# Gate integers on ScalarE, every second half's up integers on VectorE, in the last stage of a decoder layer's gated feed-forward

## The reference

```
def act_qdq(x):
    scale = jnp.maximum(jnp.max(jnp.abs(x)) / qmax, 1e-12)
    return jnp.clip(jnp.round(x / scale), -qmax - 1.0, qmax) * scale
x = act_qdq(x)
up = act_qdq(x @ lpbq_dequant(w_up).T)
gate = act_qdq(x @ lpbq_dequant(w_gate).T)
sig = fixed_qdq_u16(jax.nn.sigmoid(gate))
gate = act_qdq(gate * sig)
o = act_qdq(gate * up)
return o @ lpbq_dequant(w_down).T
```

## Time and profile before

| | |
|---|---|
| median of 3 runs | 1257.77 us (1257.39 to 1261.47) |
| the profiled execution | 1256.11 us |
| its span | 1254.3 us |
| busy in the span: PE, DVE, ACT, POOL | 91%, 85%, 74%, 36% |
| the third pass, 1102.3 to 1171.2 | 68.9 us; busy PE 55.36, DVE 62.68, ACT 33.82, POOL 49.79 |

### The profile page before, as it was taken

The page is one execution under the profiler, slowest core; times in us unless marked ns, Lnnn a source line. Parts: engine busy times, 40 slices in busy tenths (PEclk is TensorE's granted clock), DMA queues, the critical chain, the costliest instruction groups (busy, mean ns, idle before and its releaser), DMA issues. The chain is left out here.

```text
span 1254.3 us, 28844 instructions
## 1 busy us (share of the span) xinstructions
PE 1137.2 (91%) x8658; PEld 843.2 (67%) x8658; DVE 1070.1 (85%) x2303; ACT 934.0 (74%) x3155; POOL 448.1 (36%) x463
## 2 busy tenths in 40 slices
PE   1589999999999999999999999999975998989498
PEld 1456666666667666766666766666543988778498
DVE  6259999999999999999999999999874559989698
ACT  1368888888888888888888888888742569855595
POOL 0223334433334433333433333443110007767343
PEclk9899999999999999999999999999986999999799
DMA  5000000000100000100000100010000000000133
GB/s 165 23 17 27 28 22 21 21 21 23 34 22 20 20 20 20 34 24 20 20 20 20 30 29 20 20 33 22 5 4 8 1 1 0 1 1 1 32 104 99
DMA packets 35059, 32.85 MB, mean 26 GB/s; under 512 B 4164, under 2 KB 34748, under 8 KB 35004
## 3 DMA queue, kind: packets, MB, share of 16 engines
q1 hardware_dynamic: 32704, 31.50, 8.4%
q10 hardware_dynamic: 2300, 0.66, 0.3%
HBM read 24.81 MB, written 7.34 MB: 26 GB/s over the span
## 5 line engine op out<-in xcount | busy, mean ns | idle before, releaser
L593 ACT ACTIVATE Px<-score 125x896 f32<-125x896 f32 x128 | 117.4, 917 | 89.4 <-PE score L1121 89.4
L574 ACT ACTIVATE Ps<-score,nmax_s 112x112 f32<-112x112 f32 x512 | 176.3, 427 | 4.0 <-DVE nmax_s L797 4.0
L585 ACT ACTIVATE Px<-score,nmax_h 125x112 f32<-125x112 f32 x512 | 172.6, 367 | 0.8 <-DVE nmax_h L790 0.8
L790 DVE TENSOR_REDUCE nmax_c<-score 125x8 f32<-125x896 f32 x128 | 136.2, 1064 | 13.6 <-PE score L1040 10.4
L574 ACT ACTIVATION_READ_ACCUMULATOR Ps<-score,nmax_s 112x1 f32 x512 | 144.3, 282 | 0.0
L759 DVE TENSOR_REDUCE Zc<-Px 125x8 f32<-125x896 f32 x128 | 137.9, 1077 | 5.7 <-ACT Px L593 2.1
L504 POOL TENSOR_TENSOR Kbd_hi<-Ks_hi,mask 128x448 fp32r<-128x448 f32 x64 | 63.9, 999 | 202.9 <-PE score L1040 137.5
L1132 PE MATMUL outX<-Px,Vn 125*32 125x224 f32 x1536 | 113.6, 368 | 7.2 <-DVE Vn L773 7.2
L585 ACT ACTIVATION_READ_ACCUMULATOR Px<-score,nmax_h 125x1 f32 x512 | 113.0, 221 | 0.0
L525 POOL TENSOR_TENSOR rstd<-vare,half 112x1 f32<-112x1 f32 x64 | 35.1, 548 | 177.0 <-DVE vare L882 177.0
L531 POOL TENSOR_TENSOR xb<-x_in,abo 112x256 f32<-112x256 f32 x32 | 23.7, 739 | 200.2 <-DVE r L868 200.2
(11 more groups left out here) (244 smaller groups left out, 3638.2 us busy)
## 6 DMA issues: line engine op xcount, KB each, us to landing
ctx_in<-in_ctx SPq DMA_DIRECT2D x32, 375.0 KB
x_in<-in_x SPq DMA_DIRECT2D x32, 112.0 KB, 2.0
x_scratch<-x SPq DMA_DIRECT2D x32, 112.0 KB, 1.9
x2T_all<-x_scratch SPq DMA_DIRECT2D x32, 112.0 KB, 2.1
out<-x2T_all SPq DMA_DIRECT2D x32, 112.0 KB, 1.9
raw_w_up<-in_w_up SPq DMA_DIRECT2D x1, 768.0 KB, 5.6
raw_w_down<-in_w_down SPq DMA_DIRECT2D x1, 768.0 KB, 7.4
raw_w_gate<-in_w_gate SPq DMA_DIRECT2D x1, 768.0 KB, 9.5
```

Of the source, the lines that this page charges most:

```text
L574: ins = act.activation(Ps[:, g, :], score[slot][0:L, h // QUAD, (h % QUAD) * L:(h % QUAD + 1) * L], ACT.Exp, bias=nmax_s[:, g:g + 1], accu ...
L585: ins = act.activation(Px[u % 2][:, h, :], score[SLOT_OF[f"C{u}"]][0:C, h // QUAD, (h % QUAD) * L:(h % QUAD + 1) * L], ACT.Exp, bias=maxim ...
L593: act.activation(Px[u % 2][:].rearrange("s (q h) l -> s q (h l)", q=2), score[SLOT_OF[f"C{u}"]][0:C, :, 0:QW], ACT.Exp).then_inc(exp_c, 1)
L790: dve.tensor_reduce(dst, score[SLOT_OF[f"C{u}"]][0:C, :, 0:QW].rearrange("s q (h l) -> s q h l", h=QUAD), AX.X, ALU.max, negate=True).then ...
```

## The change

- ScalarE's `up_integers` serves half 0 only; VectorE gets an `up_integers` for half 1, which reads `bank[1]` itself.
- `glu_integers` goes from VectorE to ScalarE, both halves. In group 0 ScalarE first waits for `scales_ready`.
- The count of finished up integers is split by half (`up_q_done[h]`), since two engines now raise it; TensorE waits for the half whose bank it will overwrite, GpSimd likewise.

```diff
--- before.py
+++ after.py
@@ -1397,7 +1397,8 @@
         up_maxed, up_ready, scales_ready = sem("up_maxed"), sem("up_ready"), sem("scales_ready")
         gate_q_done, sig_done, sig_q_done = sem("gate_q_done"), sem("sig_done"), sem("sig_q_done")
         glu_done, glu_maxed = sem("glu_done"), sem("glu_maxed")
-        glu_q_done, up_q_done, h_done, h_maxed = sem("glu_q_done"), sem("up_q_done"), sem("h_done"), sem("h_maxed")
+        glu_q_done, h_done, h_maxed = sem("glu_q_done"), sem("h_done"), sem("h_maxed")
+        up_q_done = [sem(f"up_q_done{h}") for h in range(2)]
         TURN = HG * P
         places = {"x": spare[1][:, TURN:TURN + P], "gate": spare[1][:, TURN:TURN + P], "up": spare[1][:, TURN:TURN + P],
                   "glu": spare[0][:, TURN:TURN + P], "h": spare[1][:, TURN:TURN + P]}
@@ -1426,7 +1427,7 @@
             def hidden(g, h):
 
                 pool.wait_ge(glu_q_done, g * 2 + (h + 1))
-                pool.wait_ge(up_q_done, g * 2 + (h + 1))
+                pool.wait_ge(up_q_done[h], g + 1)
                 pool.tensor_tensor(half_of(products_of_U, g, h), glu_q[h], up_int[h], ALU.mult).then_inc(h_done, 1)
 
             def hidden_step(g, p, last):
@@ -1480,17 +1481,25 @@
                     parts(UP, g + 1, 1 - p)
                 sigmoid(g, 1)
 
-            def up_integers(g, h):
-                act.wait_ge(product, g * 2 + (HIDDEN * NH + h + 1))
+            def up_integers(g):
+                act.wait_ge(product, g * 2 + (HIDDEN * NH + 1))
+                wait(act, h_done, g * 2 - 1)
+                act.activation(up_int[0], bank[0][:, :, 0:GT], ACT.Copy, scale=tiny["up_inv"][:, 0:1])\
+                    .then_inc(up_q_done[0], 1)
+
+            def glu_integers(g, h):
                 wait(act, h_done, g * 2 + (h - 1))
-                act.activation(up_int[h], bank[h][:, :, 0:GT], ACT.Copy, scale=tiny["up_inv"][:, 0:1])\
-                    .then_inc(up_q_done, 1)
+                act.activation(glu_q[h], half_of(products_of_U, g, h), ACT.Copy, scale=tiny["glu_inv"][:, 0:1])\
+                    .then_inc(glu_q_done, 1)
 
             def hidden_step(g, p, last):
-                up_integers(g, 0)
+                up_integers(g)
+                if isinstance(g, int) and g == 0:
+                    act.wait_ge(scales_ready, 1)
+                glu_integers(g, 0)
                 if not last:
                     parts(HIDDEN, g + 1, 1 - p)
-                up_integers(g, 1)
+                glu_integers(g, 1)
 
             act.wait_ge(xpart_done, 1)
             parts(GATE, 0, 0)
@@ -1568,19 +1577,19 @@
                 else:
                     largest_glu(g, 0)
 
-            def glu_integers(g, h):
-                wait(dve, h_done, g * 2 + (h - 1))
-                dve.tensor_scalar(glu_q[h], half_of(products_of_U, g, h), tiny["glu_inv"][:, 0:1], None, ALU.mult)\
-                    .then_inc(glu_q_done, 1)
+            def up_integers(g):
+                dve.wait_ge(product, g * 2 + (HIDDEN * NH + 2))
+                wait(dve, h_done, g * 2)
+                dve.tensor_scalar(up_int[1], bank[1][:, :, 0:GT], tiny["up_inv"][:, 0:1], None, ALU.mult)\
+                    .then_inc(up_q_done[1], 1)
 
             def largest_hidden(g, h):
                 largest_of("h", products_of_U, h_done, h_maxed, g, h)
 
             def hidden_step(g, p, last):
-                glu_integers(g, 0)
                 if not isinstance(g, int) or g > 0:
                     largest_hidden(g - 1, 1)
-                glu_integers(g, 1)
+                up_integers(g)
                 largest_hidden(g, 0)
 
             top["x"].vector(dve, xmax_all[:])
@@ -1623,6 +1632,8 @@
                 if isinstance(g, int) and g == 0:
                     if freed_before is not None:
                         pe.wait_ge(freed_before, NH - 1 + h)
+                elif stage == HIDDEN:
+                    pe.wait_ge(up_q_done[h], g)
                 else:
                     pe.wait_ge(freed, g * 2 + (h - 1))
                 for m in range(h * HG, (h + 1) * HG):
@@ -1658,10 +1669,10 @@
                 products(UP, w_up, g, p, 1, up_maxed, gate_stored)
 
             def hidden_step(g, p, last):
-                products(HIDDEN, w_up, g, p, 0, up_q_done, up_maxed)
+                products(HIDDEN, w_up, g, p, 0, None, up_maxed)
                 if isinstance(g, int) and g == 0:
                     top["up"].tensor(pe)
-                products(HIDDEN, w_up, g, p, 1, up_q_done, up_maxed)
+                products(HIDDEN, w_up, g, p, 1, None, up_maxed)
                 if isinstance(g, int) and g == 0:
                     top["glu"].tensor(pe)
```

## The result

The changed kernel takes 1262.82 us in the median of six runs (1261.78 to 1264.13), the kernel before 1257.76 (1257.39 to 1261.47). The ratio is 1.0036, with an interval of 1.0023 to 1.0049: slower by 5.1 us, where 6.1 was forecast (1263.8, and 1262.82 measured).

A forecast was written before the change was run, and what follows sets the result against it. It took GpSimd's turns with VectorE (7.98 us per group) as the bound before, and an 8.51 us loop after; late group 1, slow clock 1.60 and six loops ended the stage 6.1 later: 1263.8 us, range 1259.5 to 1267.5.

The forecast's parts named there:

- VectorE and GpSimd taking turns: VectorE's gate integers block beside GpSimd's product, 2.60 us against 0.87; GpSimd idles 0.90 per half, 7.98 per group.
- The loop: TensorE half 0, up integers, gate integers, two x parts, TensorE's next half 0: 8.51 us per group, six times.
- The gate copy on ScalarE: New step between up integers and x parts, taken as 1.33 us, bounds 0.83 and 1.43.
- The start: Group 0's gate integers wait for the scales ahead of the x parts; TensorE starts group 1 at 1110.20, 4.81 us later.
- The slow matmuls: Group 1 on TensorE: the clock falls after a 4.7 us pause, adding 1.60 us, bounds 0 and 1.60.
- The end: Group 7 to VectorE's last maximum: up integers begin at 1166.84, the maximum ends at 1177.25, 6.1 us later than before.
- the first: Rival: TensorE's clock does not fall at the start; 1.60 us less, 1262.2 us; chance 0.12.
- the second: Rival: VectorE's integers queue behind GpSimd at the end; 0.8 us more, 1264.6 us; chance 0.08.
- The third: Rival: not slower, ScalarE's gate copy cheap enough to hide; 1254.2 us, or 1252.6 if the clock stays up; chance 0.12.
- The fourth: Rival: TensorE's clock falls in each group after 1.2 us pauses; six more times 1.60, 1273.4 us; chance 0.08.

The follow-up runs named there:

- the copy from SBUF: Changed kernel, VectorE making half 1's gate integers a second time from SBUF ahead of its up integers; 1265.48 us, one execution.
- the one from the bank: Changed kernel, VectorE making its up integers a second time from the bank into an unread tile; 1264.82 us, one execution.
- the pair of doubled copies: Two runs of the changed kernel, ScalarE making one half's gate integers twice: half 0 ahead of the x parts 1277.47 us, half 1 behind them 1264.11 us.
- the x parts go first: Changed kernel with ScalarE's two x parts of the next group ahead of half 0's gate integers in every group; 1256.5 us, 0.9989 of the kernel before.
- the filled pause: Changed kernel with 26 extra matmuls on TensorE in the pause ahead of group 1; 1262.26 us, 1.0032 of the kernel before.
- the run with groups 1 to 7: Changed kernel with the x parts ahead of half 0's gate integers in all groups but 0; 1259.61 us, 1.0015 of the kernel before.
- the run with gate integers 1 twice: Changed kernel, ScalarE making half 1's gate integers a second time, behind the x parts; 1264.11 us, 1.0042 of the kernel before.
- the run with gate integers 0 twice: Changed kernel, ScalarE making half 0's gate integers a second time, ahead of the x parts; 1277.47 us, 1.0154 of the kernel before.
- the run with the edit in group 0 alone: Changed kernel with the x parts ahead of the scales' wait and the gate integers in group 0 only; 1261.04 us, 1.0025 of the kernel before.

## Why the prediction was right

- **What bounded the kernel before:** VectorE and GpSimd taking turns. Right; the copy from SBUF reproduces the 0.72, the one from the bank does not. No run takes the turns alone out of the kernel before, so what they cost it by themselves is not measured.
- **The loop:** right in place, and shown by the pair of doubled copies and by the period falling when the x parts go first. Sized 8.51, measured 8.43; six times the difference, 0.46, is most of what the stage's sum was too long by (6.07 against 5.45). The gate copy on ScalarE, the term without a row, took 1.41 and a step of 1.31 (1127.31 to 1128.62); I had 1.33.
- **The start:** TensorE's group 1 began 1112.10 - 1104.24 = 7.86 after the stage's start, against 1110.20 - 1102.28 = 7.92 forecast. The slow matmuls cost 5.12 - 3.50 = 1.62, against 1.60, and the filled pause shows their cause. That the size fell so close is luck: with the same order at the start, and pauses of 4.65 and 4.64, the eighteen matmuls took 4.90 in the run with groups 1 to 7 and 6.06 in the run with gate integers 1 twice, 1.40 and 2.56 more than 3.50. The upper bound of 1.60, taken from a single fall, was too low.
- **The end:** from the up integers of group 7 to the last maximum 1178.59 - 1168.22 = 10.37, against 10.41.
- **The rivals:** the clock did fall at the start, so the first is out. VectorE's integers did not queue behind GpSimd at the end (1.62 throughout), so the second is out; the Trainium skill's rule that the two-port mode needs SBUF ("VectorE: DVE Perf Modes", section "Mode 2×_2P — use both read ports for one tensor") agrees with that 1.62. The third needed a gate copy of 0.13 to 1.04 and got 1.31. The fourth did not happen: TensorE paused 0.82 to 1.01 in groups 2 to 7 and the clock stayed 1.00. With pauses of 2.05 to 2.32 the clock fell in two of six groups of the run with gate integers 0 twice; the Trainium skill's case of a clock that swings with brief pauses ("TensorE: Matmul & The Clock Gate", section "A second HAM failure mode: psum-queue depth-cycling") comes nearer there than at the pauses of about 1 that the rival spoke of.

The median moved by 5.1 and the stage by 5.45; the rest is within the scatter outside the stage. Whether the slowing is beyond 0.3% is not settled by these runs (the interval starts at 0.23%).

## What to carry to other kernels

An engine that feeds another in a loop has a place in its queue that is on the path and a place that is free: the same copy cost 13.9 us ahead of the x parts (10.8 without the two falls of the clock) and 0.2 behind them, where the wait was longer than the copy. So before work is moved to an engine with idle time, look for what stands behind it in that queue and who waits for it. And a wait that is taken away pays only down to the next longest loop: here four bounds lay within 1.3 us of each other (8.43, 7.98, 7.74 and 7.16 per group).

## What the runs showed of the hardware that was not expected

How long TensorE paused did not tell alone whether its clock would fall. Pauses of 2.16 and 2.31 us were followed by the lower level, and pauses of 2.32 us in the same run, and of 3.22 us in the run with the edit in group 0 alone, by full clock:

```profile
1117.12 0.47 PE L1645 MATMUL gbank<-xq_hi,w_upT_hi 128*128 128x448 f32 x1 [3.22 <-ACT xq_lo L1446]
```

```profile
1117.10:1125.00 7.90, 7.47 (x36) 6.68 (x36) 5.07 (x5) 5.17 (x5) 5.59 (x3) 1.00 0.00 0
```

Ahead of the kernel before's group 0 a pause of 3.20 did make it fall. At the same place in the run with gate integers 1 twice a pause of 3.23 did not: the eighteen matmuls behind it took 3.59 from first to last start (to 1105.70).

```profile
1101.87 0.49 PE L1313 MATMUL gspare<-up_top_diag,ones 128*128 128x128 f32 x2 [3.23 <-DVE up_top_diag L1304]
1102.11 0.45 PE L1646 MATMUL gbank<-xq_hi,w_upT_hi 128*128 128x448 f32 x1
...
1105.70 0.36 PE L1648 MATMUL gbank<-xq_hi,w_upT_lo 128*128 128x448 f32 x1
```

Nor was the price of a fall one number: eighteen matmuls that take 3.50 at full clock took 4.70 to 6.06 behind the pauses after which it fell, 1.2 to 2.6 more.
